# Splitting the gate and up projections of a mixture-of-experts stage into two token halves, with four buffers for silu instead of two

## The reference, cut to what matters

```python
def body(acc, packed):
    w1e, w2e, ce = packed
    h = t @ w1e.T                         # 1024 -> 2048
    gate, up = jnp.split(h, 2, axis=-1)
    a = jax.nn.silu(gate) * up            # 1024
    o = a @ w2e.T                         # 1024 -> 1024
    return (acc + ce[:, None] * o, None)
out, _ = jax.lax.scan(body, jnp.zeros_like(t), (w1, w2, combine.T))
```

## Time and profile before

| | |
|---|---|
| median of the runs | 3269.79 us (two runs: 3220.86 and 3318.71) |
| the profiled execution | 3233.23 us, span of its slowest core 3232.2 us |
| spans of the 8 cores | 3186.0 to 3232.2 us |
| TensorE busy | 76% of the span |
| VectorE, ScalarE busy | 38%, 18% |
| DMA queue with most traffic | POOL's, 72.36 MB, 17.6% of the 16 engines' span |

### The profile page before, as it was taken

One profiled execution on the slowest core, in us unless ns is written; L12 is line 12 of the kernel. 1 busy time (PEld: TensorE's weight loads), 2 busy tenths in 40 slices (PEclk: granted clock), 3 DMA queues, 4 the chain that ended last, 5 costly groups with the idle time before them and its releaser, 6 DMA issues.

```text
span 3232.2 us, 29360 instructions; the slowest of 8 cores (3186.0 to 3232.2 us)
## 1 busy us (share of the span) xinstructions
PE 2441.2 (76%) x10564; PEld 1096.4 (34%) x10564; DVE 1223.0 (38%) x1815; ACT 590.9 (18%) x806; POOL 96.0 (3%) x113
## 2 busy tenths in 40 slices
PE   0677777755999997245888888888888888888883
PEld 0344444312444442012333333333333333333331
DVE  0677777764201214861222222222322223222236
ACT  0334444333121024220101101001010010100102
POOL 0000000000000000000000000000000000000000
PEclk9999999976999997667999999999999999999996
DMA  9000000030234214004050140410504105032012
GB/s 211 1 1 1 1 1 1 1 36 0 23 36 46 27 10 111 0 0 62 1 74 5 29 50 1 66 14 1 79 1 62 17 1 78 1 59 20 1 17 104
DMA packets 121435, 100.69 MB, mean 31 GB/s; under 512 B 102856, under 2 KB 104904, under 8 KB 118224
## 3 DMA queue, kind: packets, MB, share of 16 engines
q0 software_dynamic: 113360, 72.36, 17.6%
q1 hardware_dynamic: 7936, 26.47, 2.5%
HBM read 162.78 MB, written 8.39 MB: 53 GB/s over the span
## 4 chain that ended last, share of the span: by engine, by line
PE 59%; DVE 11%; DMA 4%; issue 3%; ACT 3%; DVEq 0%; ACTq 0%; POOLq 0%; SPq 0%
PE ps L927 14%; PE ps L937 14%; PE ps L975 12%; PE ps L700 7%; PE ps L676 7%; DVE abf L951 3%; DMA w2e<-mw 3%; PE ps L566 1%; ACT sgb L947 1%; DVE abf L954 1%; DVE y L605 1%; PE ps L568 1%; DMA w1e<-mw 1%; PE ps L595 1%; PE ps L597 1%
## 5 line engine op out<-in xcount | busy, mean ns | idle before, releaser
L927 PE MATMUL ps<-x1bf,w1e 128*128 128x512 bf16 x2048 | 502.8, 397 | 199.9 <-ACT sgb L947 139.6
L975 PE MATMUL ps<-abf,w2e 128*128 128x512 bf16 x2048 | 469.7, 394 | 67.4 <-DVE abf L954 40.8
L951 DVE TENSOR_TENSOR abf<-sgb,ps 128x512 bf16<-128x512 bf16 x256 | 174.7, 682 | 848.2 <-PE ps L937 847.8
L937 PE MATMUL ps<-x1bf,w1e 128*128 128x512 bf16 x2048 | 452.5, 379 | 0.0
L947 ACT ACTIVATE sgb<-ps 128x512 bf16<-128x512 f32 x256 | 145.9, 596 | 1484.2 <-PE ps L927 996.1
L927 PEld LDWEIGHTS ps<-x1bf,w1e 128*128 128x128 bf16 x2048 | 203.6, 101 | 490.3 <-issue 288.8
L975 PEld LDWEIGHTS ps<-abf,w2e 128*128 128x128 bf16 x2048 | 205.5, 101 | 331.6 <-issue 108.4
L990 DVE TENSOR_TENSOR y<-y,ps 128x512 f32<-128x512 f32 x256 | 158.7, 682 | 361.6 <-PE ps L975 361.6
L937 PEld LDWEIGHTS ps<-x1bf,w1e 128*128 128x128 bf16 x2048 | 200.4, 98 | 241.7
L419 ACT ACTIVATE esb<-ps,negm_s 128x1536 bf16<-128x1536 f32 x128 | 197.1, 1541 | 425.1 <-PE ps L407 425.1
L700 PE MATMUL ps<-hq,w2s 128*128 128x512 bf16 x1024 | 223.3, 381 | 10.7 <-ACT hq L684 10.7
(11 more groups left out here) (118 smaller groups left out, 1342.9 us busy)
## 6 DMA issues: line engine op xcount, KB each, us to landing
w1e<-mw POOLq DMA_DIRECT2D x8, 4096.0 KB, 29.3
w2e<-mw POOLq DMA_DIRECT2D x64, 256.0 KB, 4.6
y<-srcT SPq DMA_DIRECT2D x1, 8192.0 KB, 55.8
w2s<-w POOLq DMA_DIRECT2D x32, 256.0 KB, 5.6
src<-srcT SPq DMA_DIRECT2D x1, 8192.0 KB, 29.0
outT<-ostg SPq DMA_DIRECT2D x8, 1024.0 KB, 3.9
srcb<-srcT POOLq DMA_DIRECT2D x1, 5120.0 KB, 60.3
w1qa<-w POOLq DMA_DIRECT2D x2, 2048.0 KB, 46.5
```

The costliest lines, as they stand in the source:

```text
L927: mm = te.matmul(PS[:, tt, :], self.W1EB[:, dc, 128 * jj:128 * (jj + 1)], self.X1BF[:, dc, TT * tt:TT * (tt + 1)], start=(dc == 0), stop=( ...
L937: mm = te.matmul(PS[:, 4 + tt, :], self.W1EB[:, dc, 1024 + 128 * jj:1024 + 128 * (jj + 1)], self.X1BF[:, dc, TT * tt:TT * (tt + 1)], start ...
L951: sV.inc(ve.tensor_mul(self.ABF[:, jj, TT * tt:TT * (tt + 1)], self.SGB[:, kb, :], PS[:, 4 + tt, :]))
L975: mm = te.matmul(PS[:, bk + tt, :], self.W2E[:, sl, dffc, :], self.ABF[:, dffc, TT * tt:TT * (tt + 1)], start=(dffc == 0), stop=(dffc == D ...
```

## The change

The gate and up matmuls of a jj are no longer ordered as 32 gate then 32 up over all four token tiles, but as two halves of two token tiles: half 0 has 16 gate matmuls into banks 0 and 1 and 16 up matmuls into banks 2 and 3; half 1 the same with banks 4 and 5 and banks 6 and 7. The signals t_g and t_u are given once in each half. SGB gets four slots, one for each token tile, so that a silu waits for the multiply of the same tile in the jj before. The numbers of matmuls, silus and multiplies and their shapes stay the same. At the start of an expert after the first, TensorE waits for the last silu and multiply before the combine row, and the wait for the odd W2 evacuation (`v_bev[1]`) is dropped. Three small SBUF tiles move to make room.

```diff
@@ -68,9 +68,9 @@
 OFF_W1E = OFF_HQ + 32768
 OFF_CSB = PHASE
 OFF_CB = PHASE + 4096
-OFF_SEL = PHASE + 12288
-OFF_SG = PHASE + 14336
-OFF_W2E = PHASE + 16384
+OFF_SEL = PHASE + 8192
+OFF_SG = PHASE + 10240
+OFF_W2E = PHASE + 14336
 OFF_ROW2A = OFF_W1E
 OFF_ROW2B = OFF_W1E + 8192
 OFF_ROW2T = OFF_W1E + 16384
@@ -187,7 +187,7 @@
         self.IND = sb("ind_s", [128, 16, 8], F32, OFF_IND)
         self.GS2C = sb("gs2c_s", [128, 16], F32, OFF_GS2C)
         self.CBC = sb("cb", [128, T], BF16, OFF_CB)
-        self.SGB = sb("sgb", [128, 2, TT], BF16, OFF_SG)
+        self.SGB = sb("sgb", [128, 4, TT], BF16, OFF_SG)
         self.W2E = sb("w2e", [128, 3, DC, 128], BF16, OFF_W2E)
         self.ROW2A = sb("row2a", [1, T], F32, OFF_ROW2A)
         self.ROW2B = sb("row2b", [1, T], F32, OFF_ROW2B)
@@ -901,6 +901,8 @@
                 te.wait_ge(self.cSEL.h, 16)
             else:
                 te.wait_ge(sV.h, v_bev[0])
+                te.wait_ge(sV.h, max(v_a))
+                te.wait_ge(sS.h, max(s_sg4))
             t_cb = [0] * NTT
             for tt in range(NTT):
                 sT.inc(te.matmul(PS[:, tt, :], self.SEL8[:, 128 * e:128 * (e + 1)],
@@ -914,47 +916,51 @@
             te.wait_ge(sV.h, v_cbc)
 
             te.wait_ge(self.cW1E.h, 16 * (e + 1))
-            if e > 0:
-                te.wait_ge(sV.h, v_bev[1])
             for jj in range(DC):
-                mm = None
-                for dc in range(DC):
-                    if e == 0 and jj == 0:
-                        te.wait_ge(sS.h, self.s_x1bf[dc])
-                    for tt in range(NTT):
-                        if dc == 0:
-                            te.wait_ge(sS.h, s_sg4[tt])
-                        mm = te.matmul(PS[:, tt, :], self.W1EB[:, dc, 128 * jj:128 * (jj + 1)],
-                                       self.X1BF[:, dc, TT * tt:TT * (tt + 1)],
-                                       start=(dc == 0), stop=(dc == DC - 1))
-                sT.inc(mm)
-                t_g = sT.n
-                mm = None
-                for dc in range(DC):
-                    for tt in range(NTT):
-                        if dc == 0:
-                            te.wait_ge(sV.h, v_a[tt])
-                        mm = te.matmul(PS[:, 4 + tt, :],
-                                       self.W1EB[:, dc, 1024 + 128 * jj:1024 + 128 * (jj + 1)],
-                                       self.X1BF[:, dc, TT * tt:TT * (tt + 1)],
-                                       start=(dc == 0), stop=(dc == DC - 1))
-                sT.inc(mm)
-                t_u = sT.n
-                for tt in range(NTT):
-                    kb = tt % 2
-                    se.wait_ge(sT.h, t_g)
-                    se.wait_ge(sV.h, v_a[tt - 2] if tt >= 2 else v_a[tt + 2])
-                    sS.inc(se.activation(self.SGB[:, kb, :], PS[:, tt, :], AF.Silu))
-                    s_sg4[tt] = sS.n
-                    ve.wait_ge(sS.h, s_sg4[tt])
-                    ve.wait_ge(sT.h, t_u)
-                    sV.inc(ve.tensor_mul(self.ABF[:, jj, TT * tt:TT * (tt + 1)],
-                                         self.SGB[:, kb, :], PS[:, 4 + tt, :]))
-                    ve.wait_ge(sV.h, sV.n)
-                    sV.inc(ve.tensor_mul(self.ABF[:, jj, TT * tt:TT * (tt + 1)],
-                                         self.ABF[:, jj, TT * tt:TT * (tt + 1)],
-                                         self.CBC[:, TT * tt:TT * (tt + 1)]))
-                    v_a[tt] = sV.n
+                for half in range(2):
+                    b0 = 4 * half
+                    toff = 1024 * half
+                    mm = None
+                    for dc in range(DC):
+                        if e == 0 and jj == 0:
+                            te.wait_ge(sS.h, self.s_x1bf[dc])
+                        for tt in range(2):
+                            if dc == 0:
+                                te.wait_ge(sS.h, s_sg4[2 * half + tt])
+                            mm = te.matmul(PS[:, b0 + tt, :],
+                                           self.W1EB[:, dc, 128 * jj:128 * (jj + 1)],
+                                           self.X1BF[:, dc, toff + TT * tt:toff + TT * (tt + 1)],
+                                           start=(dc == 0), stop=(dc == DC - 1))
+                    sT.inc(mm)
+                    t_g = sT.n
+                    mm = None
+                    for dc in range(DC):
+                        for tt in range(2):
+                            if dc == 0:
+                                te.wait_ge(sV.h, v_a[2 * half + tt])
+                            mm = te.matmul(PS[:, b0 + 2 + tt, :],
+                                           self.W1EB[:, dc, 1024 + 128 * jj:1024 + 128 * (jj + 1)],
+                                           self.X1BF[:, dc, toff + TT * tt:toff + TT * (tt + 1)],
+                                           start=(dc == 0), stop=(dc == DC - 1))
+                    sT.inc(mm)
+                    t_u = sT.n
+                    for tt in range(2):
+                        kb = 2 * half + tt
+                        se.wait_ge(sT.h, t_g)
+                        se.wait_ge(sV.h, v_a[kb])
+                        sS.inc(se.activation(self.SGB[:, kb, :], PS[:, b0 + tt, :], AF.Silu))
+                        s_sg4[kb] = sS.n
+                        ve.wait_ge(sS.h, s_sg4[kb])
+                        ve.wait_ge(sT.h, t_u)
+                        sV.inc(ve.tensor_mul(
+                            self.ABF[:, jj, toff + TT * tt:toff + TT * (tt + 1)],
+                            self.SGB[:, kb, :], PS[:, b0 + 2 + tt, :]))
+                        ve.wait_ge(sV.h, sV.n)
+                        sV.inc(ve.tensor_mul(
+                            self.ABF[:, jj, toff + TT * tt:toff + TT * (tt + 1)],
+                            self.ABF[:, jj, toff + TT * tt:toff + TT * (tt + 1)],
+                            self.CBC[:, toff + TT * tt:toff + TT * (tt + 1)]))
+                        v_a[kb] = sV.n
             t_w1_end = sT.n
             if e + 1 < E:
                 ge.wait_ge(sT.h, t_w1_end)
```

## The result

The changed kernel takes 3056.27 us (median; 3045.0 to 3063.97) against 3221.70 for the kernel before, measured side by side: a ratio of 0.9476, with a 95% interval of 0.9454 to 0.9499. The forecast was 3061. The profiled execution took 3055.18 us, with core 2 as its slowest core (before: core 4).

A forecast was written before the change was run, and what follows sets the result against it. TensorE bounds the kernel, stalled in W1 by silu waits. Span 3232.2 - 156.8 - 18.7 - 4.1 + 6.7 = 3059.3; with 1.0 us outside and rounding, 3061. Forecast's own range 3049 to 3080; full range 3014 to 3148.

The forecast's parts named there:

- The silu stall: W1, TensorE's gate matmuls waiting for silu behind the two-deep SGB: goes, 56 turns x 2.80 = 156.8 us won.
- the clock behind it (18.7): W1, 29 gate matmuls running slow after 13 of the 56 turns: gone without holes, 18.7 us won.
- Weight loads and banks: W1 matmuls: load count stays, two-matmul bank return costs nothing, 0 us; rival of a slower matmul step, chance 0.04.
- The end of W1: TensorE's ABF wait shrinks 2.3 us, but the fourth w2 block, behind the next w1 load, cancels it: 0, experts 0 to 6.
- a sign of being wrong: W2 at the fourth block: a w2 block landing sooner than 30 us after W1's end would show the forecast wrong.
- The longer wait: W2, before the fourth w2 block: 5 to 9 us at each of seven experts, the largest wait of the stage.
- its clock (+6.7): W2 after the fourth-block wait: experts 4 to 6 newly lose 2.2 us of clock each, 6.7 us added.
- Expert 7: Last expert's W2, no next w1 load: 2.3 us of wait and 1.8 of clock won, 4.1 us.
- once in seven: FFN stretches after gaps of some 2.7 us lost clock once; applied to expert 7: 2.1 x 6/7 = 1.8 us.
- The block came hardly earlier: Rival at W2's fourth block: the w2 block comes earlier too, giving 3026 us; chance 0.14.
- No new stall: Rival in W1: TensorE waits each turn for a VectorE pair before up matmuls, 128 us back, 3189; chance 0.05.
- The granted clock inside W1: Rival: clock falls because holes are gone; 3148 us at 0.91, 3367 by the skill's limiter; chance 0.07.

The follow-up runs named there:

- the kernel with five slots: The changed kernel with five w2 block slots (W2E) instead of three, loaded five ahead: 3007.98 us, ratio 0.9315.

## Why the prediction was right

**The silu stall (156.8) and the clock behind it (18.7).** Right in size: 175.5 forecast, 176.1 measured over the eight W1. The quarters follow each other at 0.2158 us per matmul, and no slow piece is left inside W1 behind its first quarter, which follows a wait as before. The runs show more than the prediction said: it took slots and order as one edit, and each of them removes the stall alone. What it needs is that the last silu of a block doesn't wait for the multiplies of the same block; two ways lead there.

**Weight loads and banks (0).** Right. There are 2048 loads for the gate line's 2048 matmuls after as before, now with runs of two, so the Trainium skill's load once and multiply repeatedly ("TensorE: Matmul & The Clock Gate", Step-by-step) is not what this kernel does in either order. A bank coming back after two matmuls leaves the step at 0.2158.

**The end of W1 (0 at experts 0 to 6).** Right, and the step with the least support before: 1.5 us were won there in all. At expert 0 TensorE went on with the fourth block 1641.78 - (1612.30 - 2.70) = 32.2 us after W1's end, where it was 1662.68 - 1628.92 = 33.8 before. Over experts 0 to 6 the mean is 30.8 instead of 31.6: 5.7 us earlier in all, of which the clock of the next paragraph takes back 4.2. At expert 5 it is 29.8, just under the 30 that the prediction had named as a sign of being wrong. In the profiled executions with three slots a smaller hole ahead of W2 brought no shorter time: 3040 and 3052 us with 5 us of hole, 3055, 3057 and 3059 with 2.8, 3059 with none; with five slots the same three holes give 3034, 3008 and 2978.

**The longer wait (5 to 9 us) and its clock (+6.7).** The wait was 4.4 to 7.0, at and under the low end: the first three blocks mostly ran slow after the 2.8 us hole (22.57 us), and the fourth block came a little earlier. The clock lost in the 160 matmuls after it went from 10.2 to 14.4 us, so +4.2.

**Expert 7 (4.1).** Here the size was off: 3.0 won. The step that failed is "once in seven" for the clock after a hole of some 2.8 us. In the changed kernel's core 2, seven of the eight W2 starts lost the 1.69 us (57.10 at expert 7, 22.57 for 20.88 at six others); in the kernel with five slots all eight of its slowest core did. What seven FFN holes did on one core says little about another core or another stage.

**The total.** The span fell by 178, with 172.9 forecast. The term furthest off is experts 0 to 6, a loss of 6.7 forecast and 1.5 won; the expert stage's later start, 3.3 us, hides part of that. That the median lies within 5 us of the forecast is in part luck.

**The rivals.** The block came hardly earlier on the slowest core. On others it was nearly in time: in the changed kernel's execution cores 5 and 6 end 61 us before core 2, which had itself been the fastest core before; so it is not tied to a core. The trace shows what goes with it. Cores 0 to 3 started their first W1 within 5 us of each other (1492.2 to 1497.2), their later w1 loads landed after 25.1 to 28.4 us (median of seven) and their block waits sum to 26.7 to 39.7. Cores 4 to 7 started up to 16 us apart (1486.0 to 1502.1), with 23.2 to 23.4 and 3.6 to 10.4. That neighbours that load together slow each other fits this; no run here moves the loads apart to test it. No new stall stands in front of the up line. The granted clock inside W1 is 1.00 (80 us of the first W1 on each of the eight cores). The limiter that the Trainium skill describes (the same page, Part 1) is thus not seen in the executions compared, though TensorE is busier than before.

## What to carry to other kernels

Where two producers' buffers stall the main engine once per block, look for every way to free the slot earlier: here a buffer for each tile, or half the tiles per turn, did the same, and one of the two was enough. Before counting a gain at the front of a stage, look for the next thing in that stage with a fixed arrival; here it was a small transfer behind a large one in the same queue (at expert 0 of the kernel before it landed 33.5 us after W1's end, the large one some 30.2), and moving work in front of it was worth nothing until the small transfer was ahead by two more slots. Then two edits that had measured nothing came to 26 and 27 us.

## What was not expected of the hardware

A hole of 2.66 to 3.05 us in TensorE's work costs 1.5 to 2.9 us of slow clock or nothing, and which of the two it is stays much the same for many holes of one core, and differs between cores that run the same code in the same execution. In the trace of before, core 4 lost it at one of seven FFN holes, core 3 at six of the same seven. Three stretches of TensorE's timeline on core 3:

```profile
891.89 58.35 PE L676 MATMUL ps<-ubf,w1qb 128*128 128x512 bf16 x256 [3.05 <-DVE y L719]
952.91 56.88 PE L700 MATMUL ps<-hq,w2s 128*128 128x512 bf16 x256 [2.67 <-ACT hq L684]
...
1132.04 55.41 PE L676 MATMUL ps<-ubf,w1qb 128*128 128x512 bf16 x256 [2.80 <-DVE y L725]
```

In the kernel with five slots core 1 lost it at all eight W2 starts, core 5 of that execution at five. In the trace of before, core 3 starts the FFN stage 0.3 us ahead of core 4 (736.82 against 737.13) and comes out of it 9.6 us behind (the next matmul, L566, at 1250.79 against 1241.22), nearly all of it for these holes.
